# A fused cross-attention and FFN kernel: heads in pairs, projection banks strictly in turn, and the values weighed between a slot's transposes and its projections

## The reference

```python
h = layernorm(x)
q = h @ w_q.T + b_q;  k = ctx @ w_k.T + b_k;  v = ctx @ w_v.T + b_v     # heads of 32 features
attn = softmax(causal(q @ k.T / sqrt(32)))                               # per batch and head, 256 x 256
x = x + tanh(g_xattn) * ((attn @ v) @ w_o.T + b_o)
y = layernorm(x)
x = x + tanh(g_ffn) * (mx6(y) @ mx6(w_f).T + b_f)                        # mx6: blocks of 32, scale max/7.5, nearest of a 6-bit grid
```

## Time and profile before

| | |
|---|---|
| median of 3 executions | 1427.14 us (1426.55 to 1428.36) |
| the profiled execution | 1426.4 us, of which the span of its instructions is 1424.4 us |
| TensorE matmuls busy | 1381.7 us, 97% of the span |
| TensorE weight loads busy | 1220.1 us, 86% |
| VectorE busy | 1102.1 us, 77% |
| ScalarE busy | 894.7 us, 63% |
| GpSimd busy | 854.3 us, 60% |
| granted TensorE clock, mean | 0.989 |

### The profile page before, as it was taken

One profiled execution on the slowest core, in us unless ns is written; L12 is line 12 of the kernel. 1 busy time (PEld: TensorE's weight loads), 2 busy tenths in 40 slices (PEclk: granted clock), 3 DMA queues, 4 the chain that ended last, 5 costly groups with the idle time before them and its releaser, 6 DMA issues.

```text
span 1424.4 us, 35124 instructions
## 1 busy us (share of the span) xinstructions
PE 1381.7 (97%) x10844; PEld 1220.1 (86%) x10844; DVE 1102.1 (77%) x4219; ACT 894.7 (63%) x2969; POOL 854.3 (60%) x1387
## 2 busy tenths in 40 slices
PE   6899999999999999999999999999999999999976
PEld 6788888888888888888888888888888888888865
DVE  5778787887788878778788778788778887877763
ACT  4566666666666666666666666666666666666651
POOL 2455665566665666666656566556666566666662
PEclk9999999999999999999999999999999999999988
DMA  8444434444434444434444443444443444443310
GB/s 255 107 112 106 117 93 120 115 128 107 119 90 118 118 125 118 108 94 116 118 119 124 108 114 97 116 117 128 107 119 93 115 117 125 118 111 90 86 51 29
DMA packets 156103, 159.10 MB, mean 112 GB/s; under 512 B 28176, under 2 KB 130576, under 8 KB 155920
## 3 DMA queue, kind: packets, MB, share of 16 engines
q1 hardware_dynamic: 155920, 156.87, 41.6%
HBM read 39.33 MB, written 16.78 MB: 39 GB/s over the span
## 4 chain that ended last, share of the span: by engine, by line
PE 91%; DVE 3%; SPq 2%; issue 1%; ACT 1%; POOL 1%; DMA 1%; DVEq 0%; ACTq 0%; POOLq 0%
PE proj L483 20%; PE proj L484 20%; PE proj L485 20%; PE pT_ps L533 12%; PE oT_ps L550 6%; PE proj L577 6%; PE s_ps L522 4%; PE s_ps L523 2%; SPq L342 1%; DMA all_probs<-in_L_xattn_w_v 1%; ACT all_probs L660 1%; DVE all_probs L807 0%; DMA q_stack<-q_hi 0%; POOL x L448 0%; POOL x L444 0%
## 5 line engine op out<-in xcount | busy, mean ns | idle before, releaser
L410 POOL TENSOR_TENSOR all_probs<-all_probs,rden 128x128 f32<-128x128 f32 (+1 forms) x1024 | 505.0, 514 | 473.3 <-DVE rden L867 472.1
L660 ACT ACTIVATE all_probs<-all_probs,neg_max 128x128 f32<-128x128 f32 (+1 forms) x1024 | 458.7, 451 | 396.7 <-DVE neg_max L807 396.5
L807 DVE CUSTOM_DVE_ANT_0 all_probs<-s_ps,causal 128x128 f32<-128x128 f32 (+1 forms) x1024 | 321.7, 351 | 164.4 <-PE s_ps L523 160.8
L533 PE MATMUL pT_ps<-ident,all_probs 128*128 128x128 f32 x1536 | 264.5, 282 | 6.6 <-POOL all_probs L410 4.3
L660 ACT ACTIVATION_READ_ACCUMULATOR all_probs<-all_probs,neg_max 128x1 f32 x1024 | 195.5, 191 | 0.0
L919 DVE COPY all_probs<-pT_ps 128x384 f32<-128x384 f32 x256 | 139.0, 543 | 66.5 <-PE pT_ps L533 66.5
L533 PEld LDWEIGHTS pT_ps<-ident,all_probs 128*128 128x128 f32 x1536 | 160.4, 142 | 21.7 <-issue 12.7
L522 PE MATMUL s_ps<-k_stack,q_stack 96*128 96x256 f32 x512 | 154.8, 302 | 2.8 <-DVE neg_max L807 2.2
L483 PE MATMUL proj<-cT_hi,wk_hi 128*128 128x256 f32 x512 | 153.2, 299 | 1.9 <-DVE cT_lo L861 1.1
L483 PE MATMUL proj<-aT_hi,wq_hi 128*128 128x256 f32 x512 | 148.0, 289 | 0.4 <-ACT vs L675 0.4
L484 PE MATMUL proj<-cT_lo,wk_hi 128*128 128x256 f32 x512 | 142.4, 278 | 0.0
(11 more groups left out here) (125 smaller groups left out, 3487.3 us busy)
## 6 DMA issues: line engine op xcount, KB each, us to landing
k_stack<-k_hi SPq DMA_DIRECT2D x512, 64.0 KB, 2.0
q_stack<-q_hi SPq DMA_DIRECT2D x512, 64.0 KB, 2.1
xs<-in_x SPq DMA_DIRECT2D x32, 512.0 KB, 4.2
cs<-in_ctx SPq DMA_DIRECT2D x32, 512.0 KB, 6.1
k_stack<-k_lo SPq DMA_DIRECT2D x256, 64.0 KB, 2.0
q_stack<-q_lo SPq DMA_DIRECT2D x256, 64.0 KB, 2.1
out<-x SPq DMA_DIRECT2D x32, 512.0 KB, 3.0
vs<-in_L_xattn_w_k SPq DMA_DIRECT2D x2, 512.0 KB, 7.0
```

The source lines that it names most:

```text
L410: last = nc.gpsimd.tensor_tensor(p, p, rden[:, sd, t, h:h + 1].to_broadcast([P, (1 + t) * P]), ALU.mult)
L533: last = nc.tensor.transpose(pT_ps[h % 2][:, m * P:(m + 1) * P], probs[:, h % P_RING, m * P:(m + 1) * P], ident[:, :])
L660: last = nc.scalar.activation(probs[:, h % P_RING, cols], probs[:, h % P_RING, cols], ACT.Exp, scale=-1.0, bias=neg_max[:, sd, t, h:h + 1] ...
L807: last = nc.vector.tensor_tensor_reduce(probs[:, h % P_RING, cols], s_ps[h % 2][:, cols], causal[:, (1 - t) * P:], 1.0, MASKED, ALU.add, A ...
```

## The change

Heads go in pairs. TensorE does the scores of heads s and s+1 at the start of an even slot, then the six transposes of heads s-4 and s-3, and nothing of the kind in odd slots (`PAIR` = 2, `PT_LAG` from 3 to 4). `weigh_values` moves from slots 3 and 11 to slots 4 and 12 (`AV_LAG` 12), and from ahead of the transposes to behind them, so that it stands between the transposes and the units; `OUT_SLOTS` follow from `AV_LAG` and become 5 and 13. The ring of probabilities has six tiles, addressed by the running number of the head. VectorE takes the reciprocals of a pair in one instruction, and GpSimd divides a pair in two instructions instead of four, both in even slots. VectorE and ScalarE still do maxima and exponentials head by head; ScalarE copies the odd head's transposes in the even slot, VectorE the even head's in the odd slot that follows. The table `BANKS` goes: the units that exist are numbered in the order in which they run, over all steps, and the n-th takes bank n mod 3, so every unit waits for the unit three before it. `SLOT_PARTS` and the order of the units stay.

```diff
-PT_LAG = 3
+PAIR = 2
+PT_LAG = 4
 AV_HEADS = 2 * GROUP
-AV_LAG = 11
+AV_LAG = 12
...
-BANKS = (0, 1, 2, 0, 1, 2, 0, 1, 2, 0, 1, 2, 0, 1, 0, 2)
+BANKS = 3
...
-P_RING = 4
+P_RING = 6
...
+    in_order = [(u, i) for i in range(STEPS) for u, (_, _, lag) in enumerate(UNITS) if 0 <= i - lag < B]
+    place_of = {who: n for n, who in enumerate(in_order)}
...
-        def transposed_head(i, s):
+        def transposed_pair(i, s):
 
             lag = 2 if s >= PT_LAG else 3
             return lag, i - lag, (s - PT_LAG) % SLOTS
+
+        def prob_place(b, h):
+            return (HEADS * b + h) % P_RING
...
+        def bank_of(u, i):
+            return proj[place_of[u, i] % BANKS]
+
         def bank_before(u, i):
 
-            bank = BANKS[u]
-            while True:
-                u, i = (u - 1, i) if u else (len(UNITS) - 1, i - 1)
...
-                if BANKS[u] == bank and live(i - lag):
-                    return kind, 2 * (i - lag) + half + 1
+            n = place_of[u, i] - BANKS
+            if n < 0:
+                return None
+            kind, half, lag = UNITS[in_order[n][0]]
+            return kind, 2 * (in_order[n][1] - lag) + half + 1
...
             def divide(b, h, sd):
 
-                pool.wait_ge(rden_ok, HEADS * b + h + 1)
+                pool.wait_ge(rden_ok, HEADS * b + h + PAIR)
+                first = prob_place(b, h)
                 for t, cols in enumerate((slice(0, P), slice(P, 3 * P))):
-                    p = probs[:, h % P_RING, cols]
-                    last = nc.gpsimd.tensor_tensor(p, p, rden[:, sd, t, h:h + 1].to_broadcast([P, (1 + t) * P]),
-                                                   ALU.mult)
-                last.then_inc(div_ok, 1)
+                    p = probs[:, first:first + PAIR, cols]
+                    last = nc.gpsimd.tensor_tensor(
+                        p, p, rden[:, sd, t, h:h + PAIR].unsqueeze(2).to_broadcast([P, PAIR, (1 + t) * P]), ALU.mult)
+                last.then_inc(div_ok, PAIR)
...
                 for s in range(SLOTS):
-                    if live(i - 2):
-                        scores(i - 2, s)
+                    if s % PAIR == 0 and live(i - 2):
+                        for h in range(s, s + PAIR):
+                            scores(i - 2, h)
+                    lag, b, first = transposed_pair(i, s)
+                    if s % PAIR == 0 and live(b):
+                        for h in range(first, first + PAIR):
+                            transpose_probs(b, h)
                     if s % AV_HEADS == AV_LAG % AV_HEADS:
                         lag = 2 if s >= AV_LAG else 3
                         if live(i - lag):
                             weigh_values(i - lag, (s - AV_LAG) // AV_HEADS % 2, side(ph, lag))
-                    lag, b, h = transposed_head(i, s)
-                    if live(b):
-                        transpose_probs(b, h)
                     units(i, s)
...
-                    lag, b, h = transposed_head(i, s)
-                    if live(b) and h % 2:
+                    lag, b, first = transposed_pair(i, s)
+                    h = first + 1
+                    if s % PAIR == 0 and live(b):
 
                         act.wait_ge(pT_done, HEADS * b + h + 1)
...
-                dve.wait_ge(p_ok, HEADS * b + h + 1)
-                nc.vector.reciprocal(rden[:, sd, :, h], den[:, sd, :, h]).then_inc(rden_ok, 1)
+                dve.wait_ge(p_ok, HEADS * b + h + PAIR)
+                nc.vector.reciprocal(rden[:, sd, :, h:h + PAIR], den[:, sd, :, h:h + PAIR]).then_inc(rden_ok, PAIR)
...
-                    lag, h = (2, s - 1) if s else (3, SLOTS - 1)
-                    if live(i - lag):
+                    lag, h = (2, s - PAIR) if s else (3, SLOTS - PAIR)
+                    if s % PAIR == 0 and live(i - lag):
                         reciprocals(i - lag, h, side(ph, lag))
-                    lag, b, h = transposed_head(i, s)
-                    if live(b) and h % 2 == 0:
+                    lag, b, h = transposed_pair(i, s - s % PAIR)
+                    if s % PAIR and live(b):
 
                         dve.wait_ge(pT_done, HEADS * b + h + 1)
```

More of the change, by code:

```diff
@@ L89, in fused_kernel @@
     STACK_DMAS = 3 * GROUP // 2
-    assert T == 2 and GROUP * DK == P and KC * GROUP == HEADS and len(UNITS) == len(BANKS)
+    assert T == 2 and GROUP * DK == P and KC * GROUP == HEADS
     parts = [(u, part) for u, (kind, _, _) in enumerate(UNITS) for part in range(PARTS[kind])]
@@ L182, in fused_kernel @@
         weight_scale = {"q": SCALE, "k": 1.0, "v": 1.0, "o": gate[:, 0:1], "f": gate[:, 1:2]}
-        proj = [pb(f"proj{n}") for n in range(max(BANKS) + 1)]
+        proj = [pb(f"proj{n}") for n in range(BANKS)]
         s_ps = [pb(f"s_ps{n}") for n in range(2)]
@@ L292, in finished @@
                     yield u, kind, half, lag + (slot < ago)
+        def bank_of(u, i):
+            return proj[place_of[u, i] % BANKS]
         def bank_before(u, i):
-            bank = BANKS[u]
-            while True:
-                u, i = (u - 1, i) if u else (len(UNITS) - 1, i - 1)
-                if isinstance(i, int) and i < 0:
-                    return None
-                kind, half, lag = UNITS[u]
-                if BANKS[u] == bank and live(i - lag):
-                    return kind, 2 * (i - lag) + half + 1
+            n = place_of[u, i] - BANKS
[3 more added lines that the diff above has]
+            return kind, 2 * (in_order[n][1] - lag) + half + 1
         block = es.enter_context(nc.Block())
@@ L533, in transpose_probs @@
                     last = nc.tensor.transpose(pT_ps[h % 2][:, m * P:(m + 1) * P],
-                                               probs[:, h % P_RING, m * P:(m + 1) * P], ident[:, :])
+                                               probs[:, prob_place(b, h), m * P:(m + 1) * P], ident[:, :])
                 last.then_inc(pT_done, 1)
@@ L556, in unit @@
             def unit(u, part, kind, half, b, i):
-                bank = proj[BANKS[u]]
+                bank = bank_of(u, i)
                 if part == 0 and (before := bank_before(u, i)):
@@ L659, in exponentials @@
                 for t, cols in enumerate((slice(0, P), slice(P, 3 * P))):
-                    last = nc.scalar.activation(probs[:, h % P_RING, cols], probs[:, h % P_RING, cols], ACT.Exp,
+                    last = nc.scalar.activation(probs[:, prob_place(b, h), cols], probs[:, prob_place(b, h), cols], ACT.Exp,
                                                 scale=-1.0, bias=neg_max[:, sd, t, h:h + 1],
@@ L663, in exponentials, with unit @@
                 last.then_inc(p_ok, 1)
-            def unit(u, kind, half, b, sd):
-                bank = proj[BANKS[u]]
+            def unit(bank, kind, half, b, sd):
                 if kind in ("o", "f"):
@@ L723, in step @@
                         if live(i - lag):
-                            unit(u, kind, half, i - lag, side(ph, lag))
+                            unit(bank_of(u, i - (lag > UNITS[u][2])), kind, half, i - lag, side(ph, lag))
                     if s == OUT_SLOTS[1] and live(i - 3):
@@ L807, in maxima @@
                     last = nc.vector.tensor_tensor_reduce(
-                        probs[:, h % P_RING, cols], s_ps[h % 2][:, cols], causal[:, (1 - t) * P:], 1.0, MASKED,
+                        probs[:, prob_place(b, h), cols], s_ps[h % 2][:, cols], causal[:, (1 - t) * P:], 1.0, MASKED,
                         ALU.add, ALU.min, neg_max[:, sd, t, h:h + 1])
@@ L826, in moments, with unit @@
                                         ALU.add).then_inc(va, 1)
-            def unit(u, kind, half, b, pl, sd):
-                bank = proj[BANKS[u]]
+            def unit(bank, kind, half, b, pl, sd):
                 if kind in ("q", "k"):
@@ L925, in step @@
                         if live(i - lag):
-                            unit(u, kind, half, i - lag, place(ph, lag), side(ph, lag))
+                            unit(bank_of(u, i - (lag > UNITS[u][2])), kind, half, i - lag, place(ph, lag),
+                                 side(ph, lag))
                     if s == OUT_SLOTS[1] and live(i - 3):
```

## The result

The changed kernel takes **1430.9 us** (median of 12 executions, 1427.91 to 1432.32) against 1427.58 us (1426.42 to 1428.36) of the kernel before, run beside it: a ratio of 1.0022, with a 95% interval of 1.0015 to 1.0030. It is slower by 3.3 us; 1423.4 was predicted.

The account below looks back on a forecast made before the run. TensorE was taken as the bound, busy 1182.66 of 1183.90 us. Terms +7.7 + 2.7 - 6.3 - 7.8 = -3.7 us on 1426.4 gave 1422.7; the median 0.7 higher, 1423.4 us, range 1411 to 1436.

Parts of the forecast that it names:

- The pairs' seam: TensorE, small score followed by the next head's large score: +0.03 us for each of 256 pairs, +7.7 us.
- Rival 1: A weight load costs the same before a transpose and a score, so pairing adds 0: 1415.7 us; chance 0.2.
- The values: weigh_values behind the transposes, slots 4 and 12: same entry cost, leaving 0.04 us dearer on average for 64 calls, +2.7 us.
- The two waits: TensorE's waits of cT0 for k1's bank and of k0 for cT both go: -6.3 and -7.8 us.
- the prediction's paragraph on `k0`: k0 stops waiting for cT, as k1 is emptied earlier and the maxima of slots 0 and 1 have scores at once: -7.8 us.
- The tight place: VectorE's even-head copy in slot 7, wanted by TensorE in slot 8: fits by 0.08 us, taken as 0.
- Rival 2: VectorE's late copy stalls the transposes of slot 8 by 0.2 to 0.4 us a step: 1430 to 1436 us; chance 0.25.
- The step that failed: TensorE's work was taken as unchanged, so only seams and stalls were summed, to -3.7 us.
- the prediction's own signs: Right: both waits gone, small score to second next matmul 0.23 us, step 42.1 to 42.2 us; wrong: step over 42.3.

Follow-up runs that it names:

- the two relieved orders: Changed kernel with VectorE's odd-slot copy ahead of maxima and moments in slot 7: heads alternating, 1417.0 us; two scores then six transposes, 1430.6 us.
- Three pairs of kernels: Values ahead of against behind transposes: changed kernel 1427.9 against 1430.9 us; kernel before 1427.58 against 1429.1; alternating heads with VectorE's copy first 1411.9 against 1417.0.
- two fixes: Kernel before with banks strictly in turn, 1427.7 us; with next x normalised in slot 14 instead of 15, 1423.1 us; with both, 1414.3 us.

## Why the prediction was wrong

**The pairs' seam** was taken at +0.05 - 0.02 us per pair from one place in the first attention step. The changed trace has 0.23 us from small score to small score in place of 0.18, and the two relieved orders differ by 0.03 us a pair: right. Rival 1 (a load costs the same in front of a transpose) is out, and with it the rule of the Trainium skill's page "TensorE: Matmul & The Clock Gate", section "LDWEIGHTS (loading the stationary operand)", in so far as it makes no difference between what the load is for: from a small score to the second matmul behind it these traces have 0.05 us more than the work where another score follows, and 0.02 where a transpose does.

**The values** were given +2.7 us (64 times 0.04 is 2.6). Three pairs of kernels measure it: 3.0, then 1.5 or 2.2, then 5.1 by the medians and 3.0 by the traces. That is right within what they tell.

**The two waits** were given -6.3 and -7.8 us, each its own cause. Both went, so the sum of 0.48 us a step was right. The reason given for the first, "with distance 3 `cT0` waits for `v0`", was not: alone the banks are worth 0, in the changed kernel 0. That this term came out is luck. VectorE's list around slot 15 is one chain (the emptying of `k1`, the normalisation, the maxima of slot 0, then over ScalarE to `cT_lo`), and it fixes when `k0` can start; an earlier wait on TensorE that goes merely turns into a later one. The pairing shortened the chain: the last `cT_lo` ends 5.9 us after the first score of slot 0 in the kernel before and with the banks alone, and 4.8 in the changed kernel with either kind of banks. That VectorE would be earlier is what the prediction's paragraph on `k0` said.

**The tight place** fits in most steps, as computed, and fails in some: the small score to the transposes takes 0.109 us on average in slot 8 and 0.081 in slot 12, where 0.06 is undisturbed, and up to 0.34 in single steps. That is 0.07 us a step, 2 us. Rival 2 named place and mechanism and overrated it.

**The step that failed** is the sentence "The work itself is unchanged, so the sum is made of seams and stalls alone". The work is unchanged, its pace is not. All q and k matmuls together take 11.18 us a step in the changed trace and 10.99 before (starts to starts, less 0.085 for each early record): 0.19 us, 6 us over the kernel. With it and the tight place the sum is -3.7 + 6 + 2 = +4, and +3.3 was measured. Of the prediction's own signs the waits and the seam came out as "right", and the step, 42.39 us, as "wrong".

What sets the beat is not settled. From its fifth matmul on a run has one of two beats, with nothing between them. Of the 1456 runs of 18 or 24 matmuls in 26 steps of all fourteen traces 960 beat at 113.4 ns, and each weight load in them is recorded at 187 or 188 ns; 496 beat at 117.8 ns, and in each of them exactly a third of the loads is recorded at 190 to 193 ns. So load and matmul fall into one of two repeating patterns; the averages between these values in the table are mixtures of steps, and of the first matmuls of a run. In the changed order (two scores, then six transposes) `q1` has the slow one in every trace; with three transposes at a time it has the fast one. But `k0` behind four transposes is slow in nine of the fourteen kernels of the table, changes from step to step in four, the kernel before among them, and is fast in one, which differs from the changed kernel by a single transpose, two slots before. What puts a run into one pattern or the other was not tried; nor did any run take the slow beat away from all units. Of the 0.19 us a step the run with one transpose more gave back 0.10, all but 0.01 of what its added transpose cost. The full 6 us are counted in the traces.

## What to carry to other kernels

A wait on a bound engine is worth its length only if nothing on the same chain stands behind it: follow the late operand back before taking a wait for a gain, and do not add up single trials: here two fixes that were worth nothing and 4.8 us alone were worth 12 to 13 together. Where TensorE is the bound, put a matmul that is shorter than the next weight load in front of a transpose and not of another fp32r matmul, and when an operation's deadline moves a slot forward, reorder the list of the engine that serves it in the same change. And look at the distance from matmul to matmul in both traces, not only at the gaps: 2 ns on average on each of 96 matmuls a step undid more than the change had gained.

## What was not expected of the hardware

Two stable distances between 256-column fp32r matmuls with a weight load each, 113.4 and 117.8 ns once a run has settled, at the full granted clock (1.00) in both. The same unit, `k0`, changes from one to the other in all 26 steps when a single transpose is added some 40 matmuls and transposes earlier (117.7 ns in the changed kernel, 113.9 with the transpose). In a settled run the recorded duration of the weight loads tells which of the two it is: with the faster none reaches 190 ns, with the slower a third do. The duration also tells what a load is for: 142 ns in front of transposes, 187 to 193 in front of fp32r matmuls. Behind a 128-column score the second costs 0.05 us, the first 0.02.
